# Attention in a graph network: twenty value steps in one batch, transposes grouped 4, 2, 4, and the reciprocal of the former unit's mass behind the maximum

## What is computed

```
q = ((x @ Wq[l].T + bq[l]) * scaling).reshape(n, H, DH)
k = (x @ Wk[l].T).reshape(n, H, DH)
v = (x @ Wv[l].T).reshape(n, H, DH)
scores = jnp.einsum('ehd,ehd->eh', q[tgt], k[srcidx])
m = jax.ops.segment_max(scores, tgt, num_segments=n)
p = jnp.exp(scores - m[tgt])
s = jax.ops.segment_sum(p, tgt, num_segments=n)
w = p / (s[tgt] + 1e-16)
agg = jax.ops.segment_sum(w[:, :, None] * v[srcidx], tgt, num_segments=n)
```

## Time and profile before

| | |
|---|---|
| runs before, median of 3 | 1086.82 us (1086.33 to 1088.16) |
| the profiled execution | 1086.2 us |
| its span in the trace | 1084.4 us |
| attention of layer 1, first score load to last copy of a sum | 236.35 to 524.25 us |
| mean granted TensorE clock | 0.982 of full speed |

### The profile page before, as it was taken

How to read it: one execution, slowest core, us unless ns; L and a number is a source line. 1 busy time by engine, 2 the same in 40 slices (tenths; PEclk the granted TensorE clock), 3 DMA queues, 4 the chain that set the end, 5 groups by cost and what they waited for, 6 DMA issues and landing times. The chain is left out here.

```text
span 1084.4 us, 18765 instructions
## 1 busy us (share of the span) xinstructions
PE 1019.0 (94%) x6579; PEld 862.9 (80%) x6579; DVE 763.0 (70%) x2339; ACT 595.0 (55%) x1094; POOL 307.2 (28%) x325
## 2 busy tenths in 40 slices
PE   5899999989999999999999999899999999999943
PEld 3678777888888888888899989788888888879843
DVE  6877557568777777777489810677777777747788
ACT  7634222346666666666335632566666666652465
POOL 2000000004444444443033100344444444421303
PEclk9999999999999999999999999999999999999985
DMA  6232410577412122112303446431311211320403
GB/s 150 67 118 81 128 38 24 135 167 176 105 39 63 39 57 45 39 37 106 109 1 126 101 112 158 111 86 38 63 39 39 63 38 40 115 88 2 97 3 95
DMA packets 50758, 84.98 MB, mean 78 GB/s; under 512 B 15230, under 2 KB 33506, under 8 KB 50412
## 3 DMA queue, kind: packets, MB, share of 16 engines
q1 hardware_dynamic: 50668, 83.82, 31.1%
HBM read 36.50 MB, written 21.61 MB: 54 GB/s over the span
## 5 line engine op out<-in xcount | busy, mean ns | idle before, releaser
L1299 POOL TENSOR_SCALAR probs<-probs,mass_inv 125x1250 f32<-125x1250 f32 x160 | 210.5, 1316 | 342.4 <-DVE mass_inv L1426 342.4
L1319 PE MATMUL banks<-k_stack,q_stack 128*125 128x416 f32 (+1 forms) x960 | 298.1, 395 | 8.2 <-DVE peak L1417 5.6
L1417 DVE CUSTOM_DVE_ANT_0 probs<-banks,scores_bias 125x416 f32<-125x416 f32 (+1 forms) x480 | 267.3, 583 | 44.2 <-PE banks L1319 41.0
L1333 PE MATMUL banks<-ident,probs 125*125 125x125 f32 x1600 | 251.6, 272 | 0.9 <-ACT probs_t L1374 0.7
L1333 PEld LDWEIGHTS banks<-ident,probs 125*125 125x125 f32 x1600 | 246.4, 187 | 7.3 <-issue 2.0
L1387 ACT ACTIVATE probs<-probs,neg_peak 125x1250 f32<-125x1250 f32 x160 | 213.5, 1334 | 63.8 <-DVE neg_peak L1440 63.6
L1374 ACT ACTIVATE probs_t<-banks 125x500 f32<-125x500 f32 x320 | 151.7, 477 | 96.7 <-PE banks L1333 91.8
L1348 PE MATMUL banks<-probs_t,v_pair 125*64 125x250 f32 x1600 | 186.2, 379 | 1.2 <-ACT probs_t L1374 1.2
L1319 PEld LDWEIGHTS banks<-k_stack,q_stack 128*125 128x125 f32 x960 | 142.9, 187 | 40.3 <-DVE peak L1417 23.0
L1348 PEld LDWEIGHTS banks<-probs_t,v_pair 125*64 125x64 f32 x1600 | 108.5, 136 | 53.5 <-ACT probs_t L1374 1.5
L1408 DVE COPY probs_t<-banks 125x500 f32<-125x500 f32 x160 | 108.2, 676 | 53.8 <-PE banks L1333 53.8
(11 more groups left out here) (257 smaller groups left out, 1392.7 us busy)
## 6 DMA issues: line engine op xcount, KB each, us to landing
q_stack<-q_split SPq DMA_DIRECT2D x160, 125.0 KB, 2.3
scores_bias<-edge_bias SPq DMA_DIRECT2D x8, 1171.9 KB
edge_bias<-bias_row SPq DMA_DIRECT2D x10, 585.9 KB
k_stack<-k_lo SPq DMA_DIRECT2D x16, 312.5 KB, 4.4
resid<-residual SPq DMA_DIRECT2D x2, 2500.0 KB, 9.8
values<-v_stage SPq DMA_DIRECT2D x2, 1680.0 KB
residual<-t SPq DMA_DIRECT2D x4, 625.0 KB, 3.0
xs<-in_x SPq DMA_DIRECT2D x5, 480.0 KB
```

The lines of the kernel that those rows point to most:

```text
L1299: nc.gpsimd.tensor_scalar(probs[:, u % 4, :], probs[:, u % 4, :], mass_inv[:, u % 4:u % 4 + 1], 1.0, ALU.mult, ALU.mult).then_inc(att["pro ...
L1319: mm = nc.tensor.matmul(pb[0:NT, t % 4, 0:sn], q_stack[:, n % 2, half, part, tile * NT:(tile + 1) * NT], k_stack[:, head * N + s0:head * N ...
L1333: mm = nc.tensor.transpose(pb[0:NT, 4 + t % 3, j * NT:(j + 1) * NT], probs[:, u % 4, (j0 + j) * NT:(j0 + j + 1) * NT], ident[0:NT, 0:NT])
L1417: nc.vector.tensor_tensor_reduce(out=probs[:, slot % 4, s0:s0 + sn], in0=pb[0:NT, t % 4, 0:sn], in1=scores_bias[:, (n % GROUPS) * GROUP + ...
```

## The change

Three edits, all in the attention. `PARTS` becomes 4, 2 and 4 blocks, so that DVE's middle part has two blocks and both of ACT's parts have four. `PV_BATCHES` has one batch of twenty steps, at slot 7 of the layer and every fourth slot after it; `SLOTS` falls by two with it, and `out_of` comes two slots earlier. In DVE's list `inverted` of the former unit moves from behind the copy to behind the maximum of the present unit.

```
-        PARTS = ((0, 4), (4, 4), (8, 2))
+        PARTS = ((0, 4), (4, 2), (6, 4))
         T_LAG, PV_LAG = 3, 7
-        PV_BATCHES = {0: range(0, TILES), 2: range(TILES, 2 * TILES)}
+        PV_BATCHES = {0: range(0, 2 * TILES)}
...
                             bring(1, u, copy, PARTS)
-                        if 0 <= slot - 1 < UNITS:
-                            inverted(slot - 1)
                         if slot < UNITS:
                             scored(slot, 1)
                             scored(slot, 2)
                             dve.wait_ge(att["s_free"], 4 + 3 * slot + 3)
                             nc.vector.tensor_reduce(neg_peak[:, slot % 4:slot % 4 + 1], peak[:, slot % 4, :], AX.X, ALU.max,
                                                     negate=True).then_inc(att["neg_peak"], 1)
+                        if 0 <= slot - 1 < UNITS:
+                            inverted(slot - 1)
```

## The result

| | before | changed |
|---|---|---|
| median, 4 runs each | 1086.57 us | 1074.43 us (1072.14 to 1075.93) |
| ratio, 95% interval | | 0.9889 (0.9868 to 0.9910) |
| profiled execution | 1086.2 us | 1074.63 us (span 1072.9) |
| first score matmul to last sum, layer 1 / layer 2 | 287.86 / 287.85 | 281.86 / 281.07 |
| to the first sum | 30.50 / 30.49 | 22.83 / 22.02 |

1078.6 had been forecast with a range of 1072.5 to 1086. It came out 4 us faster than that, inside the range: -12.1 us where -8.2 was expected. Between the two profiled executions the attention accounts for -12.8 us in its two layers, and the stage before it took 1.3 more in this one execution.

A forecast was written before the change was run, and what follows sets the result against it. PE's own list and its waits for normalised probabilities were taken as the bound. Per layer, head -8.4, steady part -0.6 and tail +4.9 gave -4.1, for two layers -8.2: 1078.6 us, range 1072.5 to 1086.

The forecast's parts named there:

- What bounds it: Steady attention: PE's own list, plus 0.33 us of waiting per pass for normalised probabilities, 0.27 of it already in slot 2.
- The head: Start of a layer's attention: first sum at about 258.5 instead of 266.89, 8.4 us gained each layer.
- The pass: Steady attention: a pass of 13.91 us instead of 14.02, 0.6 us gained from first to nineteenth sum.
- from load to first transpose 0.19: Path to PE's transposes: 0.19 us between PE's load and the first transpose.
- the sum for PE alone: Steady attention: PE's own work in a pass without the wait for probabilities, 13.58 us in place of 14.02.
- DVE's copy of two: Copy of the middle two transposed blocks: holds DVE for 0.33 us, with ends at 0.26 and 0.60.
- Rival (a): DVE's copy of two blocks holds it for its full 0.41 us: +6.5 us, 1085; chance 0.1.
- The tail: End of a layer's attention: 11.2 us from nineteenth to last sum instead of 6.32, 4.9 lost.
- Rival (b): Steady passes: PE waits for nothing because hand-overs or the copy are shorter, 12 us less, 1067; chance 0.07.
- Rival (c): Slots 2 and 3: longer path over DVE and POOL, 1098 if copying two blocks costs as much as four; chance 0.08.
- Rival (d): End of a layer: clock falls to 1.2 GHz for the last batch, up to 4 us each, 1082 to 1086; chance 0.1.

The follow-up runs named there:

- split_norm: On the changed kernel, POOL's multiplication in two pieces, the first four blocks' columns first and signalled by themselves: 1060.31 us.
- batch_late: On the kernel before, one batch of twenty steps and the reciprocal behind the maximum, transposes left at 4, 4, 2: 1104.47 us.
- pre_max: On the changed kernel, the reciprocal between chunk 2 and the maximum in DVE's list: 1068.21 us.
- late_only: On the kernel before, only the reciprocal (`inverted`) moved behind the maximum: 1075.33 us, ratio 0.9888.

## Why the prediction was right, and where it was off

- **What bounds it.** Right: PE's list, then its waits for normalised probabilities in slots 2 and 3 of a pass. Reciprocal and load came at 5.74 and 7.38 as worked out. The load for slot 3 sat idle 0.16, where under 0.1 had been named; for slot 2 it was 0.30, as forecast.
- **The head.** -8.4 forecast, -7.7 and -8.5 measured; in layer 1 the clock was at its lower level from 239.0 to 242.4, which goes with the 0.8 between the layers.
- **The pass.** 13.91 forecast, 13.79 measured, 18 gaps of a layer 248.1 instead of 250.4. This is the term that was mis-sized, and most of the missing 4 us. The step "from load to first transpose 0.19", taken from rows where PE was busy, does not hold where PE had been waiting. There 309.04 (load) to 309.50 (next scores) is 0.46, where 0.19 + 0.35 = 0.54 had been put. The other 0.03 to 0.04, and the 0.08 by which the sum for PE alone was too high (13.58; split_norm has 13.50), lie in prices read to 0.01 from single rows and added some twenty times: the step from scores to transposes, put at 0.47, is mostly 0.46. Set against split_norm, PE's own list was 0.08 too dear and its waits 0.04 (0.33 forecast, 0.29 measured).
- **DVE's copy of two.** 0.33 taken, 0.33 measured. Rival (a), the full 0.41, is out, and the section of the Trainium skill that it leaned on does not ask for it, as said above.
- **The tail.** 11.2 forecast, 10.9 measured.
- **Rival (b)**, no waits at all: not in the changed kernel, but split_norm shows what it would have been, 1060, where 1067 was written.
- **Rival (c)**, the copy as dear as one of four: batch_late is that kernel. It is slower, as the rival said: 1104 where 1098 had been worked out. The rival left out that PE's four transposes delay the copy by 0.21 a pass as well, and the clock in the tails.
- **Rival (d)**, the clock in the tail: it happened in the profiled executions of pre_max, at 2.9 us a layer, and of batch_late, at 1.7 in the last batch of layer 1, and not in the changed kernel's.
- **What the prediction did not see**: how the total divides. It gave the head's gain to the reciprocal's new place alone. late_only shows that this place cuts 2.7 at the head, and 0.17 from each pass, by removing PE's short waits for DVE, which the prediction named but put under the batch. The other 5 to 6 us at the head are only the first sum coming two slots sooner, and are given back as 4.6 in the last gap; from first scores to last sum the changed kernel has 281.86 / 281.07 and late_only 282.08 in both layers. The first edit saves 0.35 a pass and loses 0.29 of it to the wait for POOL. So the third edit alone is worth all of the 12 us, the second is there to make the first bearable, and the first, as it stands, brings nothing that can be measured.

## What to carry to other kernels

Where engines hand a unit round in a ring, look first for the instruction that waits for another engine and has independent work queued behind it, and move it behind that work: here that one move was worth the whole change. Before merging work into one large piece, ask what the small pieces had been covering in the stages between them; their cover can be worth more than the entry and exit that the merger saves. And if the engine that bounds the kernel waits for a long operation of which it needs only a part at first, signal that part by itself.

## What the runs showed of the hardware

- A group of transposes that waited starts its stream sooner behind its load than one loaded behind running work: 0.08 us less up to the next group.
- An operation on DVE that waits by semaphore for the one right ahead of it starts some 0.1 us later than one that does not: 0.63 instead of 0.51 from chunk 2 to the maximum, and 0.18 from mass to reciprocal (307.22 to 307.40) instead of 0.07 from maximum to mass (307.15 to 307.22). With mass and reciprocal put into the first of these pauses, the way from chunk 2 to the next chunk 0 fell from 0.96 to 0.86.
- POOL's multiplication in two pieces costs 1.56 instead of 1.32 us.
- The clock can fall behind a hole of some us at the end of a layer in one execution (pre_max) and hold in another of nearly the same kernel (the changed one); over the last transposes and the last batch that was 2.9 us.
